# Sparse mixture of layer 1: two TensorE increments a tile instead of four, rows transposed two tiles ahead, tokens and gates copied out early, share buffers four deep

## The chip, the cores and the metric

The kernel runs on one core of one Trainium2 chip. The metric is the device time of one execution in microseconds (us). Engines are named as in the profile: PE is TensorE (PEld its weight loads), DVE VectorE, ACT ScalarE, POOL GpSimd, SP SyncE, which here only starts DMAs. A "q" behind an engine's name is its instruction sequencer.

## The reference

Two layers work on 8192 tokens (128 batches of 64) of width 128. Each layer is a cross attention to 96-wide context rows and then a mixture of experts; the outputs of both are added to x with a tanh gate. The change touches only the last of these four parts, the mixture of layer 1:

```python
def _L1_ffn_ref(x, Wg, W1, W2, W3):      # E = 8, TOP_K = 2, D = 128, H = 256
    logits = jnp.einsum('bsd,de->bse', x, Wg)
    top_vals, top_idx = jax.lax.top_k(logits, TOP_K)
    probs = jax.nn.softmax(top_vals, axis=-1)
    onehot = jax.nn.one_hot(top_idx, E, dtype=x.dtype)
    weights = jnp.einsum('bsk,bske->bse', probs, onehot)
    out = jnp.zeros_like(x)
    for e in range(E):
        u = jnp.einsum('bsd,dh->bsh', x, W1[e])
        v = jnp.einsum('bsd,dh->bsh', x, W2[e])
        h = u * jax.nn.sigmoid(u) * v
        y = jnp.einsum('bsh,hd->bsd', h, W3[e])
        out = out + y * weights[..., e][..., None]
    return out
...
    x = x + jnp.tanh(g_ffn[1]) * _L1_ffn_ref(_layernorm(x, axis=-1), ...)
```

Each token goes to two of eight experts, so there are 16384 pairs of a token and an expert.

## The kernel before

Four phases follow one another: `attention_of_layer0`, `mixture_of_layer0`, `attention_and_routing_of_layer1` and `mixture_of_layer1`. The third sorts the pairs by expert: GpSimd scatters one row of 130 floats for each pair (the normalised token, its number, its gate) into `sorted_rows` in HBM, and VectorE makes the plan `tile_row` and `tile_expert`.

`mixture_of_layer1` works through DTILES = 71 tiles of TP = 256 rows, each of one expert (HT = 2 halves of 128 rows; KH = 2 halves of the hidden width 256). A tile goes through these steps:

- SP loads its rows into `rows[t % 4]` (`load`, L1570).
- PE transposes them into the PSUM tile `tr` (L1693); DVE copies that to `xT` (L1617).
- ACT copies the expert's weights from the resident table into `w12` (L1661) and `w3` (L1664), at an address read from `tile_expert` (L1658).
- PE makes `u` and `v` (L1685, four matmuls each); ACT makes `silu` (L1656); DVE multiplies it with `v` into `hidden` (L1625).
- PE makes `y` (L1704, eight matmuls).
- DVE copies the tokens of the rows to `token`, as integers (L1633), and multiplies `y` by the gates into `shares` (L1636, two instructions).
- POOL waits for `y_ready` and starts two indirect DMAs (L1596), which scatter the shares to `contributions` in HBM at the places in `token`. These DMAs increment `kept[...]` by 16 each when they have landed.

The order on each engine is written out by hand. `tile_steps` calls `step(t, u)` with u = t % 4, the first steps and the last ones written out, the others in a hardware loop of four steps a pass. `pair_tile(t, lag)` is the tile t - lag. At step t before the change PE makes u and v of tile t-1, the transposes of tile t, and y of tile t-2, and increments a semaphore after each of the four (`u_mm`, `v_mm`, `x_transposed`, `y_mm`). DVE at step t makes xT of tile t, hidden of tile t-1, token and shares of tile t-2. `xT`, `w12`, `silu`, `hidden`, `shares`, `token` and the PSUM tiles are two deep, `rows` and `w3` four deep. Before DVE writes `token[w % 2]` it waits until the scatters of tile w-2 have landed:

```python
if not static(w) or w >= 2:
    dve.wait_ge(kept[u % 2], 16 * HT * ((w - u % 2) // 2))
dve.tensor_copy(token[u % 2][:], row[:, :, D])
```

When the last scatter has landed, SP loads the pairs of shares of each token in 16 groups (L1580), DVE adds both to X (L1644, L1646), and ACT stores X (L1669).

Of the kernel before, what the change touches and what calls it, by code (L numbers as in the profile page):

```python
# [5 lines left out]
ALU = mybir.AluOpType  # L6
# [7 lines left out]
P = 128  # L14
# [26 lines left out]
def static(t):  # L41
    return isinstance(t, int)
# [1494 lines left out]
def mixture_of_layer1(nc, sb, psum, sem, c, X, dispatch, out):  # L1537
# [17 lines left out]
    x_transposed, xT_ready, w12_ready, w3_ready = (sem(f"d_{n}") for n in ("x_transposed", "xT_ready", "w12_ready", "w3_ready"))  # L1555
    u_mm, v_mm, silu_done, h_ready, y_mm, y_ready = (sem(f"d_{n}") for n in ("u_mm", "v_mm", "silu_done", "h_ready", "y_mm", "y_ready"))
    kept = [sem(f"d_kept{i}") for i in range(2)]
    pair = [sb(f"d_pair{i}", [P, GT, 2, D], F32) for i in range(4)]
    pair_loaded = [sem(f"d_pair_loaded{i}") for i in range(4)]
    first_added, summed, stored = sem("d_first_added"), sem("d_summed"), sem("d_stored")  # L1560
    LAG = 2

    with nc.Block() as block:
        @block.sync
        def _(sp):
            def load(t, u):
                first = sp.value_load(dispatch.tile_row[0:1, bass.ds(t, 1)], min_val=0, max_val=E1 * REGION + (DUMMY_TILES - 1) * TP)
                if not static(t) or t >= 4:
# [13 lines left out]

            tile_steps(sp, 0, step)
            sp.wait_ge(kept[0], 16 * HT * (DTILES - DTILES // 2))
            sp.wait_ge(kept[1], 16 * HT * (DTILES // 2))
            for g in range(G):
                load_pair(g)
            sp.wait_ge(stored, 16 * G)

        @block.gpsimd  # L1590
        def _(pool):
            def keep(t, u):

                wait_alone(pool, y_ready, t + 1)
                for h in range(HT):
                    pool.indirect_dma_start(dispatch.contributions, bass.IndirectOffsetOnAxis(ap=token[u % 2][:, h:h + 1], axis=0),  # L1596
                                            shares[u % 2][:, h, :], None).then_inc(kept[u % 2], 16)

            def step(t, u):
                w = pair_tile(t, 2)  # L1600
                if w is not None:
                    keep(w, (u + 2) % 4)

            tile_steps(pool, LAG, step)
            pool.wait_ge(kept[0], 16 * HT * (DTILES - DTILES // 2))
            pool.wait_ge(kept[1], 16 * HT * (DTILES // 2))

        @block.vector
        def _(dve):
            def step(t, u):  # L1610
                n = pair_tile(t, 0)
                if n is not None:

                    dve.wait_ge(x_transposed, n + 1)
# [3 lines left out]
                m = pair_tile(t, 1)  # L1618
                if m is not None:

                    dve.wait_ge(silu_done, m + 1)
                    dve.wait_ge(v_mm, m + 1)
                    if not static(m) or m >= 2:
                        dve.wait_ge(y_mm, m - 1)
                    dve.tensor_tensor(hidden[1 - u % 2][:].rearrange("p k n -> p (k n)"), silu[1 - u % 2][:],  # L1625
                                      v_bank[1 - u % 2][:], ALU.mult).then_inc(h_ready, 1)
                w = pair_tile(t, 2)
                if w is not None:
                    row = rows[(u + 2) % 4]

                    if not static(w) or w >= 2:
                        dve.wait_ge(kept[u % 2], 16 * HT * ((w - u % 2) // 2))
                    dve.tensor_copy(token[u % 2][:], row[:, :, D])  # L1633
                    dve.wait_ge(y_mm, w + 1)
                    for h in range(HT):
                        last = dve.tensor_scalar(shares[u % 2][:, h, :], y[u % 2][:, bass.ts(h, D)], row[:, h, D + 1:D + 2], None,  # L1636
                                                 ALU.mult)
                    last.then_inc(y_ready, 1)

            tile_steps(dve, LAG, step)  # L1640
# [7 lines left out]
        @block.scalar  # L1648
        def _(act):
            def step(t, u):  # L1650
                n, m = pair_tile(t, 0), pair_tile(t, 1)
                if m is not None:
                    act.wait_ge(u_mm, m + 1)
                    if not static(m) or m >= 2:
                        act.wait_ge(h_ready, m - 1)
                    act.activation(silu[1 - u % 2][:], u_bank[1 - u % 2][:], ACT.Silu).then_inc(silu_done, 1)  # L1656
                if n is not None:
                    e = act.value_load(dispatch.tile_expert[0:1, bass.ds(n, 1)], min_val=0, max_val=E1 - 1)  # L1658
                    if not static(n) or n >= 2:
                        act.wait_ge(v_mm, n - 1)  # L1660
                    act.copy(w12[u % 2][:], c.w12[:, bass.ds(e, 1)].rearrange("d a i h -> d (a i h)")).then_inc(w12_ready, 1)  # L1661
                    if not static(n) or n >= 4:
                        act.wait_ge(y_mm, n - 3)
                    act.copy(w3[u][:], c.w3[:, bass.ds(e, 1)].rearrange("p a b d -> p (a b d)")).then_inc(w3_ready, 1)  # L1664

            tile_steps(act, LAG, step)
            for g in range(G):
                act.wait_ge(summed, g + 1)
                act.dma_start(out.rearrange("(t p) d -> p t d", p=P)[:, bass.ts(g, GT), :],  # L1669
                              X[:, bass.ts(g, GT), :]).then_inc(stored, 16)  # L1670

        @block.tensor
        def _(pe):
            def step(t, u):
                n = pair_tile(t, 0)
                m = pair_tile(t, 1)
                if m is not None:
                    q = 1 - u % 2
                    pe.wait_ge(xT_ready, m + 1)
                    pe.wait_ge(w12_ready, m + 1)  # L1680
                    for i, (bank, mm, done) in enumerate(((u_bank, u_mm, silu_done), (v_bank, v_mm, h_ready))):
                        if not static(m) or m >= 2:
                            pe.wait_ge(done, m - 1)
                        for k in range(KH):
                            last = pe.matmul(bank[q][:, bass.ts(k, TP)], w12[q][:, i * HID1 + k * P:i * HID1 + k * P + P],  # L1685
                                             xT[q][:], start=True, stop=True)
                        last.then_inc(mm, 1)
                if n is not None:
                    pe.wait_ge(loaded[u], 16 * ((n - u) // 4) + 16)
                    if not static(n) or n >= 2:  # L1690
                        pe.wait_ge(xT_ready, n - 1)
                    for h in range(HT):
                        last = pe.transpose(tr[u % 2][:, bass.ts(h, P)], rows[u][:, h, 0:D], c.ident[:])  # L1693
                    last.then_inc(x_transposed, 1)
                w = pair_tile(t, 2)
                if w is not None:
                    q = u % 2
                    pe.wait_ge(h_ready, w + 1)
                    pe.wait_ge(w3_ready, w + 1)
                    if not static(w) or w >= 2:  # L1700
                        pe.wait_ge(y_ready, w - 1)
                    for h in range(HT):
                        for k in range(KH):
                            last = pe.matmul(y[q][:, bass.ts(h, D)], hidden[q][:, k, bass.ts(h, P)], w3[(u + 2) % 4][:, bass.ts(k, D)],  # L1704
                                             start=(k == 0), stop=(k == KH - 1))
                    last.then_inc(y_mm, 1)

            tile_steps(pe, LAG, step)


def build(nc, a, out):
# [73 lines left out]
```

## Time and profile before

| | us |
|---|---|
| median of 3 runs | 1073.1 |
| lowest, highest | 1068.34, 1078.13 |
| the profiled execution, its own time | 1074.11 |
| its span, first to last instruction | 1072.3 |

The span is 1.8 us shorter than the execution's own time. The first transposes of the changed phase start at 766.83 us of the span, its last scatter starts at 1031.88 us, and the sums for all tokens take the rest. The start of an instruction in the trace is recorded; the end of a matmul is modelled. Engines wait at semaphores, and the releaser that stands in brackets behind a row is inferred from the semaphore events; "remote" stands where none was found.

### The profile page before, as it was taken

What the parts mean: (1) busy time and instruction counts of PE and PEld (TensorE: products, weight loads), DVE (VectorE), ACT (ScalarE), POOL (GpSimd) and SP (SyncE); (2) the same over time, 40 slices, a digit from 0 to 9 for tenths busy, and PEclk for the clock granted to TensorE, in tenths of its full rate; (3) what the DMA queues carried; (4) which work ended last, traced back from release to release, by engine and by line L of the source; (5) the groups of instructions that cost most, each with busy time, mean ns of one, the idle gap of its engine ahead of it and who ended that gap; (6) DMA issues with size and microseconds to landing.
All of it is one profiled execution on the core that took longest, in us unless ns stands there. A gap on an engine that the chain in (4) does not pass through costs nothing. (4 is left out here: it accounts for less than half of the span.)

```text
span 1072.3 us, 25830 instructions
## 1 busy us (share of the span) xinstructions
PE 829.9 (77%) x7905; PEld 607.8 (57%) x7905; DVE 680.7 (63%) x2651; ACT 522.5 (49%) x1115; POOL 452.0 (42%) x454
## 2 busy tenths in 40 slices
PE   2899999999985999996776776763388887887820
PEld 1466666666653566664554554543277776776720
DVE  3688988998895688875855464554244444444435
ACT  1577777777764455543543443442244344433400
POOL 1354544445430111101465655667355555555530
PEclk9999999999997899998966657765699999999965
DMA  4401010100000000002111111111222222222249
GB/s 116 121 20 37 17 34 17 34 17 25 11 2 2 1 0 0 0 2 72 36 48 41 48 40 42 43 38 46 82 76 77 70 73 76 71 70 69 71 154 345
DMA packets 64384, 57.47 MB, mean 54 GB/s; under 512 B 18453, under 2 KB 57901, under 8 KB 64333
## 3 DMA queue, kind: packets, MB, share of 16 engines
q1 hardware_dynamic: 46669, 34.28, 11.1%
q0 software_dynamic: 8640, 17.84, 4.7%
q10 hardware_dynamic: 9024, 4.73, 1.5%
q8 instruction: 25, 0.41, 0.2%
q14 instruction: 26, 0.21, 0.1%
HBM read 32.80 MB, written 24.02 MB: 53 GB/s over the span
## 5 line engine op out<-in xcount | busy, mean ns | idle before, releaser
L1596 POOL DMA_INDIRECT contributions<-d_y,d_token x142 | 135.9, 957 | 135.2 <-DVE d_y L1636 94.0
L1233 POOL DMA_INDIRECT sorted_rows<-r_send,r_slots x128 | 124.7, 974 | 51.4 <-issue 50.6
L1685 PE MATMUL d_u<-d_xT,d_w 128*128 128x256 f32 x284 | 80.6, 409 | 39.2 <-DVE d_xT L1617 21.5
L1656 ACT ACTIVATE d_silu<-d_u 128x512 f32<-128x512 f32 x71 | 42.4, 597 | 139.2 <-PE d_u L1685 88.1
L1617 DVE COPY d_xT<-d_tr 128x256 f32<-128x256 f32 x71 | 30.0, 423 | 120.7 <-PE d_tr L1693 57.5
L465 POOL TENSOR_SCALAR a_k_heads<-a_kT,head_of_group 128x512 f32<-128x512 f32 x60 | 92.9, 1566 | 2.7 <-ACT a_kT L510 2.7
L388 DVE TENSOR_REDUCE a_neg_max<-a_scores 128x16 f32<-128x1024 f32 x64 | 78.2, 1222 | 10.6 <-PE a_scores L619 9.1
L646 PE MATMUL a_probsT_bank<-ident,a_probs 128*128 128x128 f32 x512 | 80.5, 280 | 2.2 <-ACT a_probsT L541 0.3
L541 ACT COPY a_probsT<-a_probsT_bank 128x512 f32<-128x512 f32 x128 | 74.9, 585 | 11.3 <-PE a_probsT_bank L646 11.3
L534 ACT ACTIVATE a_probs<-a_scores 128x1024 f32<-128x1024 f32 x64 | 65.6, 1025 | 28.7 <-PE a_scores L629 28.6
L1685 PEld LDWEIGHTS d_u<-d_xT,d_w 128*128 128x128 f32 x284 | 50.7, 199 | 49.6 <-issue 21.5
L385 DVE TENSOR_REDUCE a_denom<-a_probs 128x16 f32<-128x1024 f32 x64 | 77.3, 1208 | 1.7 <-issue 1.2
L1685 PE MATMUL d_v<-d_xT,d_w 128*128 128x256 f32 x284 | 76.9, 395 | 0.0
L1704 PE MATMUL d_y_bank<-d_w,d_hidden 128*128 128x128 f32 x568 | 75.1, 275 | 0.8 <-DVE d_hidden L1625 0.8
L619 PE MATMUL a_scores<-a_k_heads,a_qT 32*64 32x256 f32 x1024 | 71.7, 395 | 2.8 <-issue 2.6
L1704 PEld LDWEIGHTS d_y_bank<-d_w,d_hidden 128*128 128x128 f32 x568 | 69.1, 192 | 1.1 <-DVE d_hidden L1625 1.0
L646 PEld LDWEIGHTS a_probsT_bank<-ident,a_probs 128*128 128x128 f32 x512 | 56.9, 141 | 17.8 <-issue 11.2
L1636 DVE TENSOR_SCALAR d_y<-d_y_bank,d_rows 128x128 f32<-128x128 f32 x142 | 43.0, 345 | 31.0 <-remote 26.3
L456 POOL TENSOR_TENSOR X<-X,out_bias 128x512 f32 (+1 forms) x16 | 20.6, 1285 | 98.8 <-ACT a_xn L497 98.8
L1685 PEld LDWEIGHTS d_v<-d_xT,d_w 128*128 128x128 f32 x284 | 56.9, 200 | 8.6
L66 POOL TENSOR_SCALAR b_rstd<-b_stats 128x4 f32<-128x4 f32 x16 | 3.7, 228 | 137.5 <-DVE b_stats L752 137.5
L1035 PE MATMUL b_h<-b_xnT,w 128*128 128x512 f32 x96 | 58.3, 694 | 0.0
(208 smaller groups left out, 1915.3 us busy)
## 6 DMA issues: line engine op xcount, KB each, us to landing
d_rows<-sorted_rows SPq DMA_DIRECT2D x71, 130.0 KB
d_pair<-contributions SPq DMA_DIRECT2D x16, 512.0 KB, 7.0
X<-in_x SPq DMA_DIRECT2D x16, 256.0 KB, 3.0
out_x<-X ACTq DMA_DIRECT2D x16, 256.0 KB, 7.4
ctxT<-in_ctx_T SPq DMA_DIRECT2D x16, 192.0 KB, 3.0
c_ctx<-in_ctx SPq DMA_DIRECT2D x16, 192.0 KB
contributions<-d_y,d_token POOLq DMA_INDIRECT x142
w<-in_L_ffn_W SPq DMA_DIRECT2D x2, 1024.0 KB
```

The lines of the kernel that those rows point to most:

```text
L385: dve.reduce_sum(denom[:], probs[u % 2][:].rearrange("p (h k) -> p h k", k=S), AX_X).then_inc(sum_done, 1)
L388: dve.tensor_reduce(neg_max[:], scores[u % 2][:].rearrange("p a (h k) -> p (a h) k", k=S), AX_X, ALU.max, negate=True).then_inc(max_done, 1)
L465: last = pool.tensor_scalar(keys_of_head(par, j), kT[:], c.head_of_group[:, j:j + 1], None, ALU.mult)
L534: act.activation(probs[(u + 1) % 2][:], scores[(u + 1) % 2][:].rearrange("p a n -> p (a n)"), ACT.Exp, scale=SCALE0).then_inc(exp_done, 1)
L541: act.copy(probsT[u % 2][:, half * HU // 2:(half + 1) * HU // 2, :].rearrange("p u q -> p (u q)"), probsT_bank[:]).then_inc(pT_ev, 1)
L619: last = pe.matmul(scores[u % 2][S * b:S * b + S, s, bass.ts(h, 4 * S)], qT[par][rows_in, h, tile, :], k_heads[par][rows_in, tile, h].rear ...
L646: last = pe.transpose(probsT_bank[:, bass.ts(k, P)], probs[u % 2][:, bass.ts(half * HU // 2 + k, P)], c.ident[:])
L1035: pe.matmul(h_bank[(C0 * par + k) % 2][:], c.w1_0[:, 2 * k:2 * k + 2, :].rearrange("d e h -> d (e h)"), xnT[par][:], start=True, stop=True ...
L1233: pool.indirect_dma_start(dispatch.rows, bass.IndirectOffsetOnAxis(ap=slots[par][:, k, j:j + 1], axis=0), send[par][k][:, j, :], None).the ...
L1596: pool.indirect_dma_start(dispatch.contributions, bass.IndirectOffsetOnAxis(ap=token[u % 2][:, h:h + 1], axis=0), shares[u % 2][:, h, :], ...
L1685: last = pe.matmul(bank[q][:, bass.ts(k, TP)], w12[q][:, i * HID1 + k * P:i * HID1 + k * P + P], xT[q][:], start=True, stop=True)
L1704: last = pe.matmul(y[q][:, bass.ts(h, D)], hidden[q][:, k, bass.ts(h, P)], w3[(u + 2) % 4][:, bass.ts(k, D)], start=(k == 0), stop=(k == K ...
```

## The change

PE keeps its work for a tile but has two increments a step instead of four: `hidden_mm` after u and v together, and `ends_mm` after the transposes and the products y of the same step. Its lags are now: transposes of tile t, u and v of tile t-2, y of tile t-3. DVE at step t makes xT of tile t-1, then token and, newly, gate of tile t-1 (`row_read` is incremented, on which SP's next load into that row buffer now waits), then the shares of tile t-4, then hidden of tile t-2. `shares` and `token` are four deep, `gate` is new and four deep, and there are four `kept` semaphores. ACT copies the weights of tile t-1 before the silu of tile t-2. POOL scatters the shares of tile t-4. Eight steps are written out ahead of the loop instead of four.

```diff
-    for t in range(4):
-        step(t, t)
-    with eng.Fori(1, DTILES // 4) as i:
+    for t in range(8):
+        step(t, t % 4)
+    with eng.Fori(2, DTILES // 4) as i:
...
-    shares = [sb(f"d_y{i}", [P, HT, D], F32) for i in range(2)]
-    token = [sb(f"d_token{i}", [P, HT], U32) for i in range(2)]
+    shares = [sb(f"d_y{i}", [P, HT, D], F32) for i in range(4)]
+    token = [sb(f"d_token{i}", [P, HT], U32) for i in range(4)]
+    gate = [sb(f"d_gate{i}", [P, HT], F32) for i in range(4)]
...
-    kept = [sem(f"d_kept{i}") for i in range(2)]
+    kept = [sem(f"d_kept{i}") for i in range(4)]
...
-    LAG = 2
+    HIDDEN, OUT, LAST = 2, 3, 4
+
+    def transposed(t):
+        return t + 1
+
+    def products(t):
+        return t + OUT + 1
...
-                    sp.wait_ge(y_ready, t - 3)
+                    sp.wait_ge(row_read, t - 3)
...
         @block.vector
         def _(dve):
+            def kept_before(tile, four):
+                dve.wait_ge(kept[four], 16 * HT * ((tile - four) // 4))
+
             def step(t, u):
...
+                n = pair_tile(t, 1)
+                if n is not None:
+                    four = (u + 3) % 4
+                    dve.wait_ge(ends_mm, transposed(n))
                     if not static(n) or n >= 2:
-                        dve.wait_ge(v_mm, n - 1)
-                    dve.tensor_copy(xT[u % 2][:], tr[u % 2][:, 0:TP]).then_inc(xT_ready, 1)
...
+                        dve.wait_ge(hidden_mm, n - 1)
+                    dve.tensor_copy(xT[four % 2][:], tr[four % 2][:, 0:TP]).then_inc(xT_ready, 1)
+                    if not static(n) or n >= 4:
+                        kept_before(n, four)
+                    dve.tensor_copy(token[four][:], rows[four][:, :, D])
+                    dve.tensor_copy(gate[four][:], rows[four][:, :, D + 1]).then_inc(row_read, 1)
+                w = pair_tile(t, LAST)
                 if w is not None:
...
+                    dve.wait_ge(ends_mm, products(w))
+                    dve.wait_ge(row_read, w + 1)
+                    if not static(w) or w >= 4:
+                        kept_before(w, u)
                     for h in range(HT):
...
+                        last = dve.tensor_scalar(shares[u][:, h, :], y[u % 2][:, bass.ts(h, D)], gate[u][:, h:h + 1], None,
                                                  ALU.mult)
                     last.then_inc(y_ready, 1)
...
+                m = pair_tile(t, HIDDEN)
+                if m is not None:
+
+                    dve.wait_ge(silu_done, m + 1)
+                    if not static(m) or m >= 2:
+                        dve.wait_ge(ends_mm, products(m - 2))
+                    dve.tensor_tensor(hidden[u % 2][:].rearrange("p k n -> p (k n)"), silu[u % 2][:],
+                                      v_bank[u % 2][:], ALU.mult).then_inc(h_ready, 1)
...
         @block.tensor
...
-                        last.then_inc(mm, 1)
+                    last.then_inc(hidden_mm, 1)
...
-                    last.then_inc(x_transposed, 1)
...
-                    last.then_inc(y_mm, 1)
...
+                if n is not None or w is not None:
+                    last.then_inc(ends_mm, 1)
```

## Rows read from the trace of the kernel before

**Rows 1.** Windows: busy us (instructions) by engine, granted clock, DMA share, GB/s

```profile
core 0: us, PE busy (x) PEld busy (x) DVE busy (x) ACT busy (x) POOL busy (x), PEclk, DMA share, GB/s
650.00:700.00 50.00, 31.57 (x208) 24.29 (x206) 27.78 (x174) 20.43 (x43) 29.45 (x30) 0.77 0.13 42
765.00:1035.00 270.00, 218.98 (x1278) 191.80 (x1278) 117.54 (x355) 109.00 (x214) 135.89 (x142) 0.95 0.23 70
```

**Rows 2.** Groups by line, 740 to 1070 us: busy, mean | idle before, releasers

```profile
L1596 POOL DMA_INDIRECT contributions<-d_y,d_token x142 | 135.9, 957 | 135.2 <-DVE d_y L1636 94.0 <-issue 40.8 <-DMA contributions<-d_y,d_token 0.3
L1625 DVE TENSOR_TENSOR d_hidden<-d_silu,d_v 128x512 f32<-128x512 f32 x71 | 48.1, 678 | 1.9 <-issue 1.6
L1636 DVE TENSOR_SCALAR d_y<-d_y_bank,d_rows 128x128 f32<-128x128 f32 x142 | 43.0, 345 | 31.0 <-remote 26.3 <-PE d_y_bank L1704 4.7
L1617 DVE COPY d_xT<-d_tr 128x256 f32<-128x256 f32 x71 | 30.0, 423 | 120.7 <-PE d_tr L1693 57.5 <-remote 32.7 <-issue 25.4
L1633 DVE CAST d_token<-d_rows 128x2 uint32<-128x2 f32 x71 | 12.3, 173 | 2.6 <-issue 1.3 <-DMA contributions<-d_y,d_token 0.4
```

**Rows 3.** Timeline of two unhindered tiles: start, us, engine, line [idle <-releaser]

```profile
854.48 1.03 PE L1685 MATMUL d_u<-d_xT,d_w 128*128 128x256 f32 x4
857.32 1.03 PE L1685 MATMUL d_u<-d_xT,d_w 128*128 128x256 f32 x4
```

**Rows 4.** Timeline, 801 to 807 us: a late stretch

```profile
801.65 1.06 PE L1704 MATMUL d_y_bank<-d_w,d_hidden 128*128 128x128 f32 x8
802.54 1.03 PE L1685 MATMUL d_u<-d_xT,d_w 128*128 128x256 f32 x4
804.93 0.61 DVE L1636 TENSOR_SCALAR d_y<-d_y_bank,d_rows 128x128 f32<-128x128 f32 x2 [1.45 <-remote]
804.99 0.60 ACT L1656 ACTIVATE d_silu<-d_u 128x512 f32<-128x512 f32 x1 [2.58 <-PE d_u L1685]
806.56 1.13 PE L1685 MATMUL d_u<-d_xT,d_w 128*128 128x256 f32 x4 [1.01 <-ACT d_w L1661]
```

**Rows 5.** Timeline, 841 to 848 us: a scatter, the token that waits, the next

```profile
841.86 0.96 POOL L1596 DMA_INDIRECT contributions<-d_y,d_token  x1 [0.30 <-issue]
844.12 0.17 DVE L1633 CAST d_token<-d_rows 128x2 uint32<-128x2 f32 x1 [0.15 <-DMA contributions<-d_y,d_token]
844.90 0.61 DVE L1636 TENSOR_SCALAR d_y<-d_y_bank,d_rows 128x128 f32<-128x128 f32 x2 [0.61 <-PE d_y_bank L1704]
846.27 0.95 POOL L1596 DMA_INDIRECT contributions<-d_y,d_token  x1 [0.93 <-issue]
847.52 0.96 POOL L1596 DMA_INDIRECT contributions<-d_y,d_token  x1 [0.30 <-issue]
```

**Rows 6.** Timeline, 1019 to 1023 us: the last waiting token

```profile
1019.36 0.95 POOL L1596 DMA_INDIRECT contributions<-d_y,d_token  x1 [0.30 <-issue]
1021.60 0.17 DVE L1633 CAST d_token<-d_rows 128x2 uint32<-128x2 f32 x1 [0.21 <-DMA contributions<-d_y,d_token]
1021.67 0.60 DVE L1636 TENSOR_SCALAR d_y<-d_y_bank,d_rows 128x128 f32<-128x128 f32 x2
```

**Rows 7.** Timeline: PE after a short and after a long idle time

```profile
820.72 1.12 PE L1685 MATMUL d_u<-d_xT,d_w 128*128 128x256 f32 x4 [1.28 <-ACT d_w L1661]
849.86 2.00 PE L1685 MATMUL d_u<-d_xT,d_w 128*128 128x256 f32 x4 [3.22 <-DVE d_xT L1617]
```

**Rows 8.** Timeline: the first and the last tiles of the phase

```profile
766.83 0.69 PE L1693 MATMUL d_tr<-ident,d_rows 128*128 128x128 f32 x2 [19.57 <-DMA d_rows<-sorted_rows]
775.69 0.60 DVE L1636 TENSOR_SCALAR d_y<-d_y_bank,d_rows 128x128 f32<-128x128 f32 x2
1027.32 0.60 DVE L1636 TENSOR_SCALAR d_y<-d_y_bank,d_rows 128x128 f32<-128x128 f32 x2
```

**Rows 9.** The chain that ended last, 1022 to 1040 us: start, us, what

```profile
1031.88 2.22 DMA contributions<-d_y,d_token
1034.11 0.38 SPq L1580
```

More of the change, by code:

```diff
@@ L1548, in mixture_of_layer1 @@
     hidden = [sb(f"d_hidden{i}", [P, KH, TP], F32) for i in range(2)]
-    shares = [sb(f"d_y{i}", [P, HT, D], F32) for i in range(2)]
-    token = [sb(f"d_token{i}", [P, HT], U32) for i in range(2)]
+    shares = [sb(f"d_y{i}", [P, HT, D], F32) for i in range(4)]
+    token = [sb(f"d_token{i}", [P, HT], U32) for i in range(4)]
+    gate = [sb(f"d_gate{i}", [P, HT], F32) for i in range(4)]
     tr, u_bank, v_bank, y = ([psum(f"d_{n}{i}", [P, 512], F32) for i in range(2)] for n in ("tr", "u", "v", "y_bank"))
     loaded = [sem(f"d_loaded{i}") for i in range(4)]
-    x_transposed, xT_ready, w12_ready, w3_ready = (sem(f"d_{n}") for n in ("x_transposed", "xT_ready", "w12_ready", "w3_ready"))
-    u_mm, v_mm, silu_done, h_ready, y_mm, y_ready = (sem(f"d_{n}") for n in ("u_mm", "v_mm", "silu_done", "h_ready", "y_mm", "y_ready"))
-    kept = [sem(f"d_kept{i}") for i in range(2)]
+    xT_ready, row_read, w12_ready, w3_ready = (sem(f"d_{n}") for n in ("xT_ready", "row_read", "w12_ready", "w3_ready"))
+    hidden_mm, ends_mm, silu_done, h_ready, y_ready = (sem(f"d_{n}") for n in ("hidden_mm", "ends_mm", "silu_done", "h_ready", "y_ready"))
+    kept = [sem(f"d_kept{i}") for i in range(4)]
     pair = [sb(f"d_pair{i}", [P, GT, 2, D], F32) for i in range(4)]
@@ L1583, in _ @@
             tile_steps(sp, 0, step)
-            sp.wait_ge(kept[0], 16 * HT * (DTILES - DTILES // 2))
-            sp.wait_ge(kept[1], 16 * HT * (DTILES // 2))
+            for u in range(4):
+                sp.wait_ge(kept[u], 16 * HT * len(range(u, DTILES, 4)))
             for g in range(G):
@@ L1595, in keep @@
                 for h in range(HT):
-                    pool.indirect_dma_start(dispatch.contributions, bass.IndirectOffsetOnAxis(ap=token[u % 2][:, h:h + 1], axis=0),
-                                            shares[u % 2][:, h, :], None).then_inc(kept[u % 2], 16)
+                    pool.indirect_dma_start(dispatch.contributions, bass.IndirectOffsetOnAxis(ap=token[u][:, h:h + 1], axis=0),
+                                            shares[u][:, h, :], None).then_inc(kept[u], 16)
             def step(t, u):
-                w = pair_tile(t, 2)
+                w = pair_tile(t, LAST)
@@ L1601, in step @@
                 if w is not None:
[L1602 to L1606, printed above, removed]
+                    keep(w, u)
+            tile_steps(pool, LAST, step)
+            for u in range(4):
+                pool.wait_ge(kept[u], 16 * HT * len(range(u, DTILES, 4)))
         @block.vector
         def _(dve):
+            def kept_before(tile, four):
+                dve.wait_ge(kept[four], 16 * HT * ((tile - four) // 4))
@@ new lines, in step @@
+                w = pair_tile(t, LAST)
+                if w is not None:
+                    dve.wait_ge(ends_mm, products(w))
+                    dve.wait_ge(row_read, w + 1)
+                    if not static(w) or w >= 4:
+                        kept_before(w, u)
+                    for h in range(HT):
+                        last = dve.tensor_scalar(shares[u][:, h, :], y[u % 2][:, bass.ts(h, D)], gate[u][:, h:h + 1], None,
+                                                 ALU.mult)
+                    last.then_inc(y_ready, 1)
@@ L1619, in step @@
+                m = pair_tile(t, HIDDEN)
                 if m is not None:
                     dve.wait_ge(silu_done, m + 1)
-                    dve.wait_ge(v_mm, m + 1)
                     if not static(m) or m >= 2:
[L1624 to L1638, printed above, removed]
@@ L1640, in _ @@
-            tile_steps(dve, LAG, step)
+                        dve.wait_ge(ends_mm, products(m - 2))
+                    dve.tensor_tensor(hidden[u % 2][:].rearrange("p k n -> p (k n)"), silu[u % 2][:],
+                                      v_bank[u % 2][:], ALU.mult).then_inc(h_ready, 1)
+            tile_steps(dve, LAST, step)
             for g in range(G):
@@ L1650, in step @@
             def step(t, u):
-                n, m = pair_tile(t, 0), pair_tile(t, 1)
+                n, m = pair_tile(t, 1), pair_tile(t, HIDDEN)
+                if n is not None:
+                    four = (u + 3) % 4
+                    e = act.value_load(dispatch.tile_expert[0:1, bass.ds(n, 1)], min_val=0, max_val=E1 - 1)
+                    if not static(n) or n >= 2:
+                        act.wait_ge(hidden_mm, n - 1)
+                    act.copy(w12[four % 2][:], c.w12[:, bass.ds(e, 1)].rearrange("d a i h -> d (a i h)")).then_inc(w12_ready, 1)
+                    if not static(n) or n >= 4:
+                        act.wait_ge(ends_mm, products(n - 4))
+                    act.copy(w3[four][:], c.w3[:, bass.ds(e, 1)].rearrange("p a b d -> p (a b d)")).then_inc(w3_ready, 1)
                 if m is not None:
-                    act.wait_ge(u_mm, m + 1)
+                    act.wait_ge(hidden_mm, m + 1)
                     if not static(m) or m >= 2:
                         act.wait_ge(h_ready, m - 1)
[L1656 to L1666, printed above, removed]
+                    act.activation(silu[u % 2][:], u_bank[u % 2][:], ACT.Silu).then_inc(silu_done, 1)
+            tile_steps(act, LAST, step)
             for g in range(G):
@@ L1674, in step @@
             def step(t, u):
-                n = pair_tile(t, 0)
-                m = pair_tile(t, 1)
+                m = pair_tile(t, HIDDEN)
                 if m is not None:
-                    q = 1 - u % 2
+                    q = u % 2
                     pe.wait_ge(xT_ready, m + 1)
                     pe.wait_ge(w12_ready, m + 1)
-                    for i, (bank, mm, done) in enumerate(((u_bank, u_mm, silu_done), (v_bank, v_mm, h_ready))):
+                    for i, (bank, done) in enumerate(((u_bank, silu_done), (v_bank, h_ready))):
                         if not static(m) or m >= 2:
@@ L1686, in step @@
                                              xT[q][:], start=True, stop=True)
-                        last.then_inc(mm, 1)
+                    last.then_inc(hidden_mm, 1)
+                n = pair_tile(t, 0)
                 if n is not None:
@@ L1693, in step @@
                         last = pe.transpose(tr[u % 2][:, bass.ts(h, P)], rows[u][:, h, 0:D], c.ident[:])
-                    last.then_inc(x_transposed, 1)
-                w = pair_tile(t, 2)
+                w = pair_tile(t, OUT)
                 if w is not None:
-                    q = u % 2
+                    q = 1 - u % 2
                     pe.wait_ge(h_ready, w + 1)
@@ L1703, in step @@
                         for k in range(KH):
-                            last = pe.matmul(y[q][:, bass.ts(h, D)], hidden[q][:, k, bass.ts(h, P)], w3[(u + 2) % 4][:, bass.ts(k, D)],
+                            last = pe.matmul(y[q][:, bass.ts(h, D)], hidden[q][:, k, bass.ts(h, P)], w3[(u + 1) % 4][:, bass.ts(k, D)],
                                              start=(k == 0), stop=(k == KH - 1))
-                    last.then_inc(y_mm, 1)
-            tile_steps(pe, LAG, step)
+                if n is not None or w is not None:
+                    last.then_inc(ends_mm, 1)
+            tile_steps(pe, OUT, step)
 def build(nc, a, out):
```

3 lines of the change are left out of this document (removed).

## The prediction

> **What bounds the kernel now.** I read the busy time by stretch first: in the 270 us of the sparse mixture PE is busy 219 us at a granted clock of 0.95, while DVE, ACT and POOL stay at 118, 109 and 136 us [rows 1]. PE is nearest to a bound, but it isn't one throughout. The timeline shows what a tile costs when nothing hinders it: from one group of u matmuls to the next 2.84 us, with PE never idle [rows 3]. The shares of the first tile begin at 775.69 and those of the last at 1027.32, which is 251.6 us for 70 steps, or 3.60 us a step [rows 8]. So about 0.75 us a step, some 53 us in all, are stalls.
>
> The timeline shows where they come from. The products y that started at 801.65 end, by the model, at 802.71, and the u matmuls at 803.57; but the shares that need the one and the silu that needs the other start at 804.93 and 804.99, together, 2.2 and 1.4 us late [rows 4]. Both wait for PE increments alone. Behind this the weight copy comes late, and the next u starts at 806.56, after an idle time of 1.01 us. The groups count 31 us of idle time before the shares, 26 of them with no releaser found, and 121 us before xT, in which DVE's plain waiting for the next transposes is contained [rows 2]; in the timeline such a place is found again about every second tile. This is what the change is aimed at.
>
> The second thing to read is the scatter. POOL's two indirect DMAs of a tile start 1.25 us apart (846.27, 847.52) and take 0.96 us each [rows 5], 2.5 us of POOL for a tile, and at 3.60 us a step they are hidden. What counts is how long one takes to land. The token copy of tile w waits for the scatters of tile w-2. In row 844.12 it is released 2.26 us after the start of the second of them (841.86) [rows 5], in row 1021.60 2.24 us after it (1019.36) [rows 6]. Over all 69 tokens that have such a wait, the shortest distance from that scatter's start is 2.24 us, and 12 of the 69 lie between 2.24 and 2.28 us: that is a floor, the landing. The last scatter confirms it with 2.22 us, until SP is released [rows 9]. Now this wait costs DVE only 0.4 us in all [rows 2], because two steps (7.2 us) lie between the shares of w-2 and the token of w.
>
> **The change, part by part.** *Two increments instead of four, and more lag on PE.* PE's instructions stay the same: 2.84 us a tile. xT of a tile is now made a whole step before its u; u and v are made a step before y, as before. A late increment of up to 2.4 us then mostly falls into slack. If nothing else stood in the way, this would give back most of the 53 us. That silu now waits for v too costs about 1 us of slack (v is four matmuls of the same shape as u, 1.03 us in row 802.54 [rows 4]), and hidden still has until the y of the next step. I price the fewer increments themselves at nothing on the path, from 0 to -53 us by the stalls above; which end holds doesn't matter if the next part decides.
>
> The Trainium skill ("TensorE: Matmul & The Clock Gate", The cost: per-tile semaphore tail) says that increments on matmuls serialise at about 26 ns each. By that figure, two fewer on 71 tiles would be an estimated 3.7 us, and no row here shows such a small term by itself; the late ones in [rows 4] are more than fifty times as long.
>
> *Tokens and gates early, four buffers.* This decides. DVE at step t copies the token of tile t-1, in buffer (t-1) % 4. It must first wait until the scatters that read this buffer have landed: those of tile t-5. The shares of tile t-5 are made at DVE's step t-1 (lag 4). So the token copy of step t waits for scatters that could only be started after the shares of step t-1. Before, two steps lay between the two; now it is one, since the token is copied three steps ahead of its use and the buffers only grew by two. Queued behind the waiting copy on DVE stand the gate copy, the shares of tile t-4 and hidden of t-2, and for those wait POOL and PE. So a ring closes, once in every step:
>
> - shares end to first scatter start: 846.27 less 845.51 (844.90 + 0.61) is 0.76; in the rows where POOL was idle it is always 0.75 to 0.78. I take 0.75 [rows 5].
> - first to second scatter start: 1.26, the pitch in the groups (957 ns busy and 0.30 between) [rows 2, 5].
> - second scatter start to release of the token copy: 2.25 [rows 5, 6].
> - token start to shares start: 0.07 [rows 6], and another 0.07 for the gate copy, which the trace before doesn't have; the nearest row is the token's own. Bounds: 0 (wholly overlapped) and 0.78, the distance from 844.12 to 844.90 [rows 5], which may hold sequencer work for the waits between. I take 0.14, since in row 1021.60 a token that was really held back let the shares follow after 0.07.
> - both shares: 0.60 [rows 6].
>
> Together 5.00 us a step. The other work fits beside it: xT, hidden (0.42 and 0.68 [rows 2]) run while DVE would wait anyway, PE's 2.84 us and POOL's 2.5 us are shorter, ACT needs 1.5 us (109.0 over 71 tiles [rows 1]). PE's late increments have over 2 us of room in such a step, so they cost nothing more.
>
> *Lags, SP, prologue.* SP's load now waits for `row_read`, three steps ahead of the transposes: hidden. One more step of lag at the start: u and v of tile 0 start at 768 as before, then silu comes after v, hidden, y behind the next tile's u and v; I put the end of the first shares at 776.7 instead of 776.29 [rows 8]. Eight steps written out instead of four: nothing, from 0 to 1 us.
>
> **The sum.** The ring holds for the tokens of tiles 4 to 70, 67 times. 776.7 + 67 x 5.00 = 1111.7 is then the end of the shares of tile 67. The shares of 68 to 70 are held by no token copy, so POOL sets the pace: eight scatters from 1112.45 on, 1.26 apart, the last started at 1121.3 and landed 2.24 later, at 1123.5. Before, this was 1034.1 [rows 9]. The sums behind it stay as they are. The change costs 89.4 us: 1074.1 + 89.4 = 1163.5 against the profiled execution's own time, and against the median, which lies 1.0 lower, 1162.5. I say 1163.
>
> **The rivals.** *Faster: PE becomes the bound.* If the token copy never waited, a step would be 2.84 to 2.95 us and the 70 steps would save 70 x 0.65 to 0.75, about 50 us: 1024. For it speak PE's stalls and the slack that the new lags give. It would decide if the copy reached one step further back: 0.75 + 1.26 + 2.25 is 4.3 us, and fits in two steps of 2.84. Against it: the indices of the diff say one step. Even scatters that landed the moment their instruction ends (0.96 us instead of 2.25) would give 3.71 us a step, no better than the 3.60 of now. Chance 0.03.
>
> *No change.* A ring of about 3.6 us needs a landing 0.85 us after the scatter's start, shorter than the instruction. Chance 0.02.
>
> *Slower still: the PE clock.* In a step of 5.00 us PE would be idle some 2.1 us. After an idle time of 1.28 us the u matmuls kept their 1.12 us; after 3.22 us they took 2.00 us, half speed (1.2 instead of 2.4 GHz) [rows 7]. 2.1 us lies between. Where PE had regular gaps, from 650 to 700 us, the mean granted clock was 0.77 [rows 1]. At half speed a tile takes 5.7 us and PE is the bound of the step; held throughout, 67 x 0.7 gives 47 us more, 1210. But a slow tile has no gap, after which the clock was back within two tiles at 854.48 [rows 3, 7], and the 2.1 us of slack take up one slow tile's first half. I expect 0 to 20 us from it. With the upper bound of 0.78 us between token and shares the ring is 5.64 us and the time 1206. Both together are the case "slower than 1185": chance 0.12. The forecast, 1145 to 1185, has 0.83.
>
> **How the numbers follow.** Forecast 1163. Ring pieces read from floors can hardly be shorter: without the gate's 0.07 and with 2.22 for the landing it is 4.90, 1156; I go to 1150. Upwards the range takes in half the clock's price and most of the bound of the waits: 1195. About 1 in 10 is left above, less below. About 1 per cent, 11 us, is what a measurement of this kernel can tell from no change: faster 0.03, same 0.02, slower 0.95.
>
> **What the profile of the changed kernel would show.** The token copy's idle time, 0.4 us before, becomes the largest wait of DVE, well over 100 us, released by the scatter DMAs. Token starts lie 5.0 us apart, each 2.25 us after the second scatter of tile t-5. PE is idle about 2 us in each step and waits for hidden ahead of y. POOL waits for the shares each time. The windows give PE at 57% to 65% busy over a phase of some 360 us instead of 270. I am wrong if token starts lie 2.9 us apart, if the release comes from PE, or if the granted clock falls to 0.6 in the phase and the tile, not the ring, sets the step.

## The result, and the profile after

The changed kernel takes 1168.2 us (median of 4 runs, 1163.82 to 1170.14) against 1071.09 us for the kernel before on the same chip (median of 4, with one run more than the table of before has): a ratio of 1.089, with a 95% interval of 1.0841 to 1.094. The forecast was 1163, with a range of 1150 to 1195. The profiled execution took 1170.14 us, its span is 1168.1 us.

The waits of the whole execution, largest first (engine, line, what it waited for: total us, times, longest), show at once which part decided:

```profile
DVE d_token L1630 <- DMA contributions<-d_y,d_token: 225.5, 67, 5.2
ACT d_silu L1676 <- PE d_v L1696: 222.5, 69, 6.7
POOL contributions L1603 <- DVE d_y L1639: 202.6, 67, 16.4
...
PE d_y_bank L1715 <- DVE d_hidden L1648: 73.7, 62, 3.7
```

The token copy waited 0.4 us before [rows 2]; now it waits 225.5 us, 67 times, once for each of the tiles 4 to 70. POOL waits for DVE as often as DVE waits for POOL's DMAs. That is a ring seen from both sides. In this phase no wait is left whose releaser is "remote"; in the routing phase ahead such waits stand much as before, the largest with 46.9 us in 10 places (48.5 in 11 in the kernel before):

```profile
ACT c_xnT L1395 <- remote: 46.9, 10, 5.8
```

The timeline of two steps (start, us, engine, line; idle time and releaser in brackets) has the pieces of the ring one behind the other:

```profile
900.53 1.94 PE L1715 MATMUL d_y_bank<-d_w,d_hidden 128*128 128x128 f32 x8 [1.86 <-DVE d_hidden L1648]
900.63 0.96 POOL L1603 DMA_INDIRECT contributions<-d_y,d_token  x1 [2.82 <-DVE d_y L1639]
901.89 0.96 POOL L1603 DMA_INDIRECT contributions<-d_y,d_token  x1 [0.30 <-issue]
902.26 1.91 PE L1696 MATMUL d_u<-d_xT,d_w 128*128 128x256 f32 x4
...
904.16 0.17 DVE L1630 CAST d_token<-d_rows 128x2 uint32<-128x2 f32 x1 [3.35 <-DMA contributions<-d_y,d_token]
904.24 0.16 DVE L1631 COPY d_gate<-d_rows 128x2 f32<-128x2 f32 x1
904.31 0.60 DVE L1639 TENSOR_SCALAR d_y<-d_y_bank,d_gate 128x128 f32<-128x128 f32 x2
904.83 0.68 DVE L1648 TENSOR_TENSOR d_hidden<-d_silu,d_v 128x512 f32<-128x512 f32 x1
905.42 0.42 DVE L1627 COPY d_xT<-d_tr 128x256 f32<-128x256 f32 x1
905.67 0.96 POOL L1603 DMA_INDIRECT contributions<-d_y,d_token  x1 [2.81 <-DVE d_y L1639]
...
906.55 1.03 PE L1696 MATMUL d_u<-d_xT,d_w 128*128 128x256 f32 x4
906.93 0.96 POOL L1603 DMA_INDIRECT contributions<-d_y,d_token  x1 [0.30 <-issue]
...
909.18 0.17 DVE L1630 CAST d_token<-d_rows 128x2 uint32<-128x2 f32 x1 [3.34 <-DMA contributions<-d_y,d_token]
```

From 904.16: shares 0.15 later and 0.60 long, end at 904.91; first scatter at 905.67, 0.76 later; second at 906.93, 1.26 later; next token copy at 909.18, 2.25 later. Together 5.02. From 905.84 to 909.18 DVE has nothing to do, and from 907.89 on neither has POOL. Over the whole ring phase the median distance of two token copies is 5.01 us. The last rows of the phase answer to [rows 9]:

```profile
1127.47 0.95 POOL L1603 DMA_INDIRECT contributions<-d_y,d_token  x1 [0.31 <-issue]
1129.83 10.25 SPq L1587 DMA_DIRECT2D d_pair<-contributions  x8
```

The last scatter lands at about 1129.8 instead of 1034.1; the first transposes start at 768.02 instead of 766.83. The windows of the phase show a lower clock and PE far from a bound (the columns as in [rows 1]):

```profile
765.00:1130.00 365.00, 270.13 (x1278) 222.76 (x1278) 119.96 (x426) 109.18 (x214) 135.90 (x142) 0.84 0.16 52
```

### The profile page after: what moved, and what is told of

Read it like the earlier page. It is cut to its first block and busy times, and to the rows that moved or that the text cites. A ratio compares the mean times of both kernels' runs of the same rounds, so it can differ in the third digit from the quotient of the medians.

```text
span 1168.1 us, 25868 instructions
## 1 busy us (share of the span) xinstructions
PE 877.9 (75%) x7905; PEld 635.3 (54%) x7905; DVE 683.4 (59%) x2722; ACT 522.0 (45%) x1115; POOL 451.0 (39%) x454
## 5 line engine op out<-in xcount | busy, mean ns | idle before, releaser
L1715 PE MATMUL d_y_bank<-d_w,d_hidden 128*128 128x128 f32 x568 | 93.5, 315 | 83.2 <-DVE d_hidden L1648 73.7
L1630 DVE CAST d_token<-d_rows 128x2 uint32<-128x2 f32 x71 | 12.0, 169 | 225.5 <-DMA contributions<-d_y,d_token 225.5
L1715 PEld LDWEIGHTS d_y_bank<-d_w,d_hidden 128*128 128x128 f32 x568 | 78.4, 214 | 100.3 <-DVE d_hidden L1648 72.0
L1696 PE MATMUL d_u<-d_xT,d_w 128*128 128x256 f32 x284 | 96.8, 476 | 0.0
L1696 PE MATMUL d_v<-d_xT,d_w 128*128 128x256 f32 x284 | 87.8, 439 | 0.0
L1696 PEld LDWEIGHTS d_v<-d_xT,d_w 128*128 128x128 f32 x284 | 66.9, 236 | 13.6
L1696 PEld LDWEIGHTS d_u<-d_xT,d_w 128*128 128x128 f32 x284 | 62.1, 242 | 7.1
L1668 ACT COPY d_w<-w 128x512 f32 x71 | 43.9, 618 | 33.9 <-PEq L1203 18.7
```

## The experiments

All of them leave the computation as it is, except that one scatters half of the shares a second time. They ran in four groups, and in each group the kernel before was timed on the same chip: it took 974.5 us (chip 0), 973.7 (chip 3), 1073.4 (chip 11) and 973.9 (chip 3 again, 28 minutes after its first time). The number of the chip of the first result isn't known. These figures fall into two kinds, 974 and 1072, which the text calls two kinds of chip; that the time goes by the chip, and not by a state that a chip can leave, rests on chip 3 alone, which gave 974 both times. A time is to be read against the kernel before of its own group.

| run | what | before, same group | time | ratio, 95% interval |
|---|---|---|---|---|
| e1_token_lag2 | copies of tile t-2 | 974.52 | 971.99 | 0.9966 (0.9943 to 0.999) |
| e2_four_incs | e1, four PE increments | 974.52 | 973.05 | 0.9988 (0.9966 to 1.0009) |
| e3_before_one_token | before, one token buffer | 974.52 | 1126.07 | 1.1554 (1.1513 to 1.1596) |
| e4_three_scatters | changed, third scatter | 974.52 | 1206.16 | 1.2416 (1.2369 to 1.2464) |
| before_again | before, a profile | 973.68 | 978.5 (one run) | |
| after_again | changed | 973.68 | 1121.58 | 1.1486 (1.1441 to 1.1531) |
| e1_again, e2_again | as above | 973.68 | 972.60, 971.84 | 0.9984, 0.9976 |
| e5_shares_first | changed, shares ahead of copies | 1073.44 | 1051.63 | 0.9808 (0.9766 to 0.985) |
| e6_copies_last | changed, copies at the end | 1073.44 | 1059.89 | 0.9862 (0.9819 to 0.9904) |
| e1_third, e2_third | as above | 973.85 | 974.27, 973.78 | 0.9993, 0.9989 |

**e1_token_lag2: the copies one step later.** Theory: the ring. Rivals: the longer lags or the clock cost the time; or the ring is gone and the old stalls return.

```diff
-                    if not static(n) or n >= 4:
-                        kept_before(n, four)
-                    dve.tensor_copy(token[four][:], rows[four][:, :, D])
...
+                r = pair_tile(t, 2)
+                if r is not None:
+                    four = (u + 2) % 4
+                    if not static(r) or r >= 4:
+                        kept_before(r, four)
+                    dve.tensor_copy(token[four][:], rows[four][:, :, D])
```

> The changed kernel with one edit: DVE copies tokens and gates of tile t-2 instead of t-1, so two steps lie between the shares of a tile and the copy that reuses its token buffer. Ring theory: two steps have to hold 4.3 us plus the 0.7 us of DVE work, so the ring no longer sets the step; PE's 2.84 us does, with a little left over: 2.85 to 3.1 us a step and 1020 to 1040 us. Rival (the longer lags, the gate copy or the lower PE clock cost the time, not the ring): at least 1130 us. Rival (ring gone, but the old stalls are back): 3.6 us a step, about 1070 us.

Measured: 971.99 us. The expected figures were reckoned against 1071 us, which this chip doesn't have; the step is what to compare. Nor can this run decide the second rival: on this kind of chip the kernel before has no such stalls that could return (before_again, below). Two u groups of its timeline:

```profile
820.89 1.03 PE L1699 MATMUL d_u<-d_xT,d_w 128*128 128x256 f32 x4
...
823.73 1.03 PE L1699 MATMUL d_u<-d_xT,d_w 128*128 128x256 f32 x4
```

2.84 us a step, PE without a pause. The lags, the gate copy, the deeper buffers and the two increments are all still in, so none of them costs the 148 us that the changed kernel loses on this kind of chip (after_again), and the one step does.

**e2_four_incs.** e1 with two more increments a tile on a semaphore that nobody waits for.

```diff
+                        if i == 0:
+                            last.then_inc(spare, 1)
                     last.then_inc(hidden_mm, 1)
...
+                if n is not None and w is not None:
+                    last.then_inc(spare, 1)
```

> The kernel of e1 with two more PE increments a tile, after u and after the transposes, on a semaphore that nobody waits for. If the number of increments makes them late, the stalls come back in part: over 10 us slower than e1. If it is only the slack of the new lags that hides them, within 3 us of e1.

Measured: 973.05 us, 1.1 us above e1, and in the two repeats 0.8 and 0.5 us below it. On this kind of chip two increments a tile more or less can't be measured.

**e3_before_one_token: the ring alone, in the kernel before.**

```diff
-    token = [sb(f"d_token{i}", [P, HT], U32) for i in range(2)]
+    token = [sb("d_token0", [P, HT], U32)] * 2
...
+                    if not static(w) or w >= 1:
+                        dve.wait_ge(kept[1 - u % 2], 16 * HT * ((w + 1 - (1 - u % 2)) // 2))
```

> The kernel before with one token buffer instead of two, so that the token copy of tile w waits for the scatters of tile w-1, one step back, and nothing else of the change. Ring theory: 0.75 + 1.26 + 2.25 + 0.07 + 0.60 = 4.93 us a step instead of 3.60, 70 times 1.33 is 93 us more: about 1165 us. Rival (the slowdown needs the new lags): under 1100 us.

Measured: 1126.07 us, within 5 us of the changed kernel on such a chip (1121.58). The expected 1165 was again reckoned from 1071; on this chip 151.6 us were lost instead of 93, about 70 times the difference between this ring and the 2.84 us that a step of the kernel before takes here. Its waits and two of its steps:

```profile
DVE d_token L1635 <- DMA contributions<-d_y,d_token: 240.0, 70, 5.3
```

```profile
852.28 0.17 DVE L1635 CAST d_token<-d_rows 128x2 uint32<-128x2 f32 x1 [3.41 <-DMA contributions<-d_y,d_token]
852.36 0.60 DVE L1638 TENSOR_SCALAR d_y<-d_y_bank,d_rows 128x128 f32<-128x128 f32 x2
853.71 0.96 POOL L1596 DMA_INDIRECT contributions<-d_y,d_token  x1 [2.79 <-DVE d_y L1638]
854.98 0.96 POOL L1596 DMA_INDIRECT contributions<-d_y,d_token  x1 [0.30 <-issue]
857.22 0.17 DVE L1635 CAST d_token<-d_rows 128x2 uint32<-128x2 f32 x1 [3.34 <-DMA contributions<-d_y,d_token]
```

4.94 us here, without the gate copy (expected: 4.93). Over all steps the median is 5.00, since in this kernel the landing takes a little longer: 2.24 to 3.73 us over the 70 rings, with a median of 2.30, and why isn't known. Nothing of the change is in this kernel but the distance of one step between shares and token copy, and that makes the whole slowdown. One token buffer at no lag and four buffers three steps early are the same ring.

**e4_three_scatters: one term of the ring doubled.** The changed kernel, with the second half of each tile's shares scattered once more, to a tensor that nobody reads.

```diff
-                for h in range(HT):
-                    pool.indirect_dma_start(dispatch.contributions, ...
+                for place, h in ((dispatch.contributions, 0), (dispatch.contributions, 1), (dispatch.spare, 1)):
+                    pool.indirect_dma_start(place, ...
```

> The changed kernel with a third scatter a tile (the second half once more, to a tensor of its own that nobody reads). Ring theory: one more pitch of 1.26 us in each of 67 rings, 84 us more than the changed kernel, and 1.26 us each for the last four tiles: about 1257 us. Rival (a wait for transfers or bandwidth sets the step, POOL's issue time does not): under 1210 us.

Measured: 1206.16 us, 84.6 above after_again's 1121.58 on the same kind of chip; 67 times 1.26 is 84.4. (The 1257 and the rival's 1210 in the expectation were reckoned from 1168; on this kind of chip both lie 47 us lower, and the time is above the rival's.) The median distance of two token copies is 6.27 us instead of 5.02. The last four tiles, with 1.26 us more each, should have brought another 5 us, so 89. From the first transposes to the last scatter the two profiles differ by 86.8 us (445.7 against 358.9), and ahead of this phase by 5 us the other way. POOL's timeline shows the term itself:

```profile
852.55 0.96 POOL L1604 DMA_INDIRECT contributions<-d_y,d_token  x1 [2.83 <-DVE d_y L1640]
853.81 0.95 POOL L1604 DMA_INDIRECT contributions<-d_y,d_token  x1 [0.30 <-issue]
855.07 0.96 POOL L1604 DMA_INDIRECT spare_contributions<-d_y,d_token  x1 [0.30 <-issue]
857.35 0.17 DVE L1631 CAST d_token<-d_rows 128x2 uint32<-128x2 f32 x1 [4.65 <-DMA spare_contributions<-d_y,d_token]
```

**before_again and after_again**, both unedited, to see the two kinds of chip.

> The kernel before, unedited, to have its profile from the same chip as the experiments, where its time was 974.5 us and not 1071. If the late PE increments (waits of DVE and ACT whose releaser is remote or a matmul that had long ended) belong to the chip and not to the kernel, and this is the chip of the first experiments: a step of 2.9 us, no remote waits, 970 to 978 us. If it is the chip of the first result: 3.6 us a step and 1068 to 1078 us.

> The changed kernel, unedited. The ring has no term that the late increments touch, so a step stays at 5.01 us wherever it runs. On the chip where the kernel before takes 974 us: 67 times 5.01 less 2.84 is 145 us more, 1120 us. On the other: 1168 us.

Measured: 978.5 and 1121.58 us. The ring doesn't know the chip: the median distance of two token copies is 5.01 us in the first profile of the changed kernel and 5.02 us here. The kernel before does. Its waits between 730 and 930 us hold no "remote", and PE's u groups follow one another every 2.84 us:

```profile
ACT d_silu L1656 <- PE d_u L1685: 86.5, 70, 3.2
DVE d_xT L1617 <- PE d_tr L1693: 79.8, 67, 3.7
```

```profile
821.79 1.03 PE L1685 MATMUL d_u<-d_xT,d_w 128*128 128x256 f32 x4
822.85 0.60 ACT L1656 ACTIVATE d_silu<-d_u 128x512 f32<-128x512 f32 x1 [1.19 <-PE d_u L1685]
824.63 1.03 PE L1685 MATMUL d_u<-d_xT,d_w 128*128 128x256 f32 x4
```

The silu starts 0.03 us after the u group's modelled end (822.82); in [rows 4] it was 1.42. Counted over the phase, no silu of this profile is more than 0.12 us late where ACT was idle, against 21 of 71 in the first one of the kernel before, 0.7 to 2.5 us late each.

**e1_again, e2_again.**

> The kernel of e1 (tokens and gates of tile t-2). On the chip where the kernel before takes 974 us: 972 us again. On the chip where it takes 1071 us: if the longer lags hide the late increments, 2.9 to 3.1 us a step in this phase, which saves 35 to 50 us: 1020 to 1035 us; if the late increments are too frequent to be hidden, 1060 to 1075 us.

> The kernel of e2 (e1 with two more PE increments a tile that nobody waits for). On the chip where the kernel before takes 974 us: within 3 us of e1. On the other: if each increment carries a chance to be late, over 10 us above e1; if the number of increments is nothing to it, within 3 us.

Measured: 972.60 and 971.84 us; the chip was of the 974 kind again.

**e5_shares_first and e6_copies_last: the place in DVE's queue.** Both keep the copies of tile t-1 and their wait of one step. e5 moves them behind the shares of t-4, e6 behind hidden as well, to the end of the step.

```diff
-                    if not static(n) or n >= 4:
-                        kept_before(n, four)
-                    dve.tensor_copy(token[four][:], rows[four][:, :, D])
-                    dve.tensor_copy(gate[four][:], rows[four][:, :, D + 1]).then_inc(row_read, 1)
...
                     last.then_inc(y_ready, 1)
+                if n is not None:
+                    four = (u + 3) % 4
+                    if not static(n) or n >= 4:
+                        kept_before(n, four)
+                    dve.tensor_copy(token[four][:], rows[four][:, :, D])
+                    dve.tensor_copy(gate[four][:], rows[four][:, :, D + 1]).then_inc(row_read, 1)
```

> The changed kernel with one move: in DVE's step the token and gate copies of tile t-1 stand behind the shares of tile t-4 and ahead of hidden, no longer ahead of the shares. The copy still waits for the scatters of tile t-5, but the shares of t-4 are no longer queued behind it, so from shares over scatter and copy to the next shares behind the copy there are two steps: 4.26 + 0.14 + 0.65 (hidden) + 0.35 (xT) + 0.60, together 6.0 us for two, 3.0 a step. Ring theory: 67 x 0.16 above PE's 2.84: 975 to 990 us (where the kernel before takes 974). Rival (the wait itself costs, wherever it stands, since it is one step behind its shares): 1121 us as the changed kernel.

> As e5, with the token and gate copies at the very end of DVE's step, behind hidden. The same two steps now hold 4.26 + 0.14 + 0.35 + 0.60, 5.35 us or 2.7 a step, less than PE's 2.84: the time of e1, 969 to 975 us, and 5 to 15 us less than e5. Rival (place in the queue is nothing to it): 1121 us, the same as e5.

Measured: 1051.63 and 1059.89 us on a chip where the kernel before takes 1073.44 and the changed one, by the first result, 1168. The rival is out: the wait of one step doesn't cost the 97 us when the next shares don't stand behind it in the queue. It isn't gone, though; the token copies still wait for the scatters (e5, then e6):

```profile
DVE d_token L1642 <- DMA contributions<-d_y,d_token: 75.4, 40, 3.4
DVE d_token L1650 <- DMA contributions<-d_y,d_token: 30.2, 22, 3.2
```

From first to last shares a step takes 3.28 us in e5, where 3.0 was forecast, and 3.43 in e6, where it was to be PE's 2.84. The order of the two was forecast wrong: e6 is the slower one. PE increments are late here, also with two of them a tile, as in e5 between 856 and 862 us:

```profile
858.47 1.03 PE L1698 MATMUL d_v<-d_xT,d_w 128*128 128x256 f32 x4
...
859.66 1.16 PE L1717 MATMUL d_y_bank<-d_w,d_hidden 128*128 128x128 f32 x8
861.05 0.42 DVE L1627 COPY d_xT<-d_tr 128x256 f32<-128x256 f32 x1 [1.45 <-PE d_y_bank L1717]
861.14 0.60 ACT L1678 ACTIVATE d_silu<-d_u 128x512 f32<-128x512 f32 x1 [1.43 <-remote]
```

v ends by the model at 859.50, silu starts 1.64 us later. That isn't the model alone: y, which PE starts only behind v, has its recorded start at 859.66, 1.48 us ahead of silu. Of the silus before which ACT was idle, 35 of 70 were over 0.4 us late in e5, with up to 2.7 us, and 37 of 69 in e6, with up to 5.2 us. Their lateness sums to 46.5 and 65.3 us. Why e6 has the longer ones isn't settled.

**e1_third, e2_third**, to have e1 and e2 on a chip with late increments.

> The kernel of e1 once more, for a chip on which PE increments are late (there the kernel before takes 1071 to 1073 us). On such a chip the two sisters of e1 took 1052 and 1060 us; with the ring at two steps and 5.0 us, less than PE's 5.7, e1 should be no slower than the better of them: 1040 to 1055 us. If the lags of the change hid nothing, 1070 us. On a chip without late increments 972 us.

> The kernel of e2 (e1 with two more PE increments a tile, that nobody waits for). If late increments come with their number, so that four a tile are late more often than two, over 10 us above e1 on a chip with late increments; if they come with PE's dense work alone, within 3 us. On a chip without late increments within 3 us.

Measured: 974.27 and 973.78 us; the chip was of the 974 kind, so what e1, and two increments more, do on the other kind stays open.

## Why the prediction was right

**The ring of one step.** Right, and shown from both sides: taking it away alone (e1) gives the kernel before's time, and putting it alone into the kernel before (e3) gives the changed kernel's within 5 us, both on the 974 kind of chip. Its terms were 0.75, 1.26, 2.25, 0.14 and 0.60; the timeline has 0.76, 1.26, 2.25, 0.15 and 0.60. The gate copy's 0.07, taken from the nearest row, came out as 0.08 and 0.07 (904.16, 904.24, 904.31), and its bound of 0.78 was far off. That it is the queue behind the wait that closes the ring is what e5 shows. The total, not the step, hangs on the chip: the sum starts at 766.83 us and was compared with a kernel before of 1071, both of one kind of chip. On the other kind the same kernel takes 1121.58 us, under the range, and loses 148 us instead of 97, at the same 5.02 us a step.

**The sum.** 89.4 us were forecast; the profile has 95.8 (1168.1 less 1072.3). The missing 6.4 us don't lie in the usual ring: 1.2 are the earlier phases (768.02 against 766.83) and 0.3 the prologue; 1.05 the first ring, in which the landing took 3.27 us from 780.20; 1.8 a single pause of POOL between the two scatters of a tile, 2.12 us of idle time instead of 0.30; 0.3 the last ring; the rest is 67 times 0.01 or 0.02 and the tail.

```profile
1064.39 0.96 POOL L1603 DMA_INDIRECT contributions<-d_y,d_token  x1 [2.12 <-issue]
```

This pause could have been read ahead. It stands ahead of the 114th scatter of the phase in every profile of this case, that of the kernel before too (978.91, then 982.08, 3.17 us instead of 1.26). In e4, with three scatters a tile, it is again the 114th (2.20 us behind the 113th), so it goes by the count of scatters and not by the tile. What it is no run shows.

**The clock.** The step was priced at 0 to 20 us and cost nothing. The granted clock fell to 0.84 over the phase, so half speed did come: the y group at 900.53 took 1.94 us and the u group behind it 1.91, against 1.16 at 905.56 and 1.03 at 906.55. PE had been idle for 1.86 us before the first, less than the 3.22 of [rows 7]. But the slow tile used up slack only: the token copies at 904.16 and 909.18 keep their 5.02 us, and in all 67 rings the shares start 0.14 to 0.17 us after the token copy, so never waited for PE. The forecast of 57% to 65% PE busy was too low for the same reason, it is 74% (270 of 365 us), half-speed matmuls being longer and the waits of PE shorter.

**Late increments.** The reading was right for the chip of the profile, and so was its consequence that they would cost nothing in a step of 5 us: in the changed kernel no silu is more than 0.12 us late. What hiding them would gain, 53 us at the far end and 1024 us in the rival "PE becomes the bound", stays open. Where the chip has them, e5 and e6 gained 22 and 14 us, not 50. Half of the silus were still late there and the token copies still waited, and the two shares aren't separated. Where it has none, the kernel before is at 2.84 us a step already and e1 was 2.5 and 1.1 us faster and 0.4 us slower in three comparisons. The first one's interval leaves out 1, the other two don't. The Trainium skill ("TensorE: Matmul & The Clock Gate", The cost: per-tile semaphore tail) has about 26 ns for an increment, an estimated 3.7 us for two a tile. It didn't show: e2 less e1 is +1.1, -0.8 and -0.5 us.

The better kernel of this case is thus the changed one with the copies moved. e5 is 1.9% faster than the kernel before on the one kind of chip (interval 1.5% to 2.3%), e1 ties with the kernel before on the other. Neither was run on both.

## What to carry to other kernels

Count buffers by the distance between the last use of a tile in a slot and the first write of the next, in steps, and not by their number. Copying three steps earlier eats three of four buffers. If the release goes over an engine that starts a DMA and over its landing, add up that way (here 4.3 us) and see that it fits into the steps between.

A wait in an in-order queue costs what stands behind it. Putting the same wait behind the work that starts the next round (e5) lets two steps pass from one round of shares to the next that depends on it; the step fell from 5.0 to 3.3 us.

A stall read in one profile may belong to the chip it was taken on. Time the kernel before anew beside every experiment, and compare steps, not totals.

## What the runs showed of the hardware that was not expected

The same kernel takes 974 us on two chips and 1072 us on one or two others, with a spread of about 1% within a kind. The profiles put 53 of these 97 us in this phase (first to last shares: 198.8 us in before_again, 251.6 in the first profile [rows 8]) and 44 ahead of it (first transposes at 722.7 and 766.8). In this phase PE is idle 46 us in the one and 6 in the other, and the rest is longer matmuls (busy 219 against 207 us, at a granted clock of 0.95 and 0.97). What the two profiles differ in is that ACT and DVE start late behind PE: a silu up to 2.5 us after the modelled end of its matmuls, an xT copy up to 3.6 us, in e6 a silu 5.2 us. The text calls these late increments; what is seen is the late start of the waiter. They came only on the one kind of chip, and with two increments a tile as well as with four. In the changed kernel's steps, with 0.2 to 2 us of PE idle ahead of y, there was none; but the routing phase of the same profile, where PE is busy 35 of 50 us, has the "remote" waits of ACT, so pauses alone don't keep them away. No profile from the 974 kind of chip has a "remote" wait anywhere. What delays them no run here shows.

An indirect scatter of 128 rows of 512 B released its waiter 2.23 to 2.28 us after it started in all 67 rings of after_again, more than half of it after the instruction had ended (0.96 us). The median is 2.24 us in the first profile of the changed kernel and 2.25 here.

PE's clock fell to half (1.2 instead of 2.4 GHz) in some of the changed kernel's steps, in which pauses of about 1.9 and 0.2 us ahead of y alternate for long stretches: after one idle time of 1.86 us, at 900.53, the y group took 1.94 us. After another of 1.91 us, at 890.48, it took 1.16, so the length of the last pause doesn't decide it alone.
